# Turning normed rows, K and Q by VectorE blocks and SBUF transfers instead of TensorE

## The reference

```
# layers 0 and 1 (H = 16 and 8 heads), for each batch
xn = layernorm(x) * w + b
q, k, v = xn @ Wq + bq, xn @ Wk + bk, xn @ Wv + bv     # k masked by rows
q = softmax(q over a head's columns);  k = softmax(k over the 512 rows);  v = v * keep
attn = k^T v  per head;  y = q attn
x = x + silu(layernorm(y) * gain + shift) @ Wo + bo
# layer 2: softmax attention, 16 heads (not touched)
# layer 3: two norms and a modulation, then projections of the normed rows
#   (dlt, B, C, mx), then two state-space scans over 512 steps (not touched)
```

## Time and profile before

| | |
|---|---|
| median of three runs | 5686.29 us |
| the profiled execution | 5681.6 us |
| its span | 5679.5 us |
| TensorE, VectorE, ScalarE, GpSimd busy | 95%, 74%, 51%, 51% |
| layer 0, start of V of the first batch | 232.68 us |
| layer 1, start of V of the first batch | 840.14 us |
| front layer, first product | 2598.28 us |
| first product over the whole row with the scan | after 2915 us |

### The profile page before, as it was taken

How to read it: one execution, slowest core, us unless ns; L and a number is a source line. 1 busy time by engine, 2 the same in 40 slices (tenths; PEclk the granted TensorE clock), 3 DMA queues, 4 the chain that set the end, 5 groups by cost and what they waited for, 6 DMA issues and landing times. The chain is left out here.

```text
span 5679.5 us, 136465 instructions
## 1 busy us (share of the span) xinstructions
PE 5410.8 (95%) x58478; PEld 3262.1 (57%) x58478; DVE 4209.2 (74%) x5904; ACT 2919.1 (51%) x4944; POOL 2906.6 (51%) x956
## 2 busy tenths in 40 slices
PE   8999989998999999978989999999999999999998
PEld 3555545554455555544445566666666666666665
DVE  1456545554466666673349999999999999999996
ACT  0122212222455555551247776777777677677774
POOL 0000000000000000003449999999999999999997
PEclk9999999999999999998999999999999999999999
DMA  6200021001000000004431111112111121201211
GB/s 237 80 34 33 32 71 34 31 29 65 11 1 20 17 21 17 21 20 164 167 120 50 52 34 62 65 60 69 54 43 55 60 67 54 73 24 62 65 59 33
DMA packets 146330, 321.90 MB, mean 57 GB/s; under 512 B 27721, under 2 KB 28362, under 8 KB 135514
## 3 DMA queue, kind: packets, MB, share of 16 engines
q1 hardware_dynamic: 142866, 308.25, 16.1%
q10 hardware_dynamic: 2896, 5.34, 0.3%
HBM read 238.66 MB, written 74.89 MB: 55 GB/s over the span
## 5 line engine op out<-in xcount | busy, mean ns | idle before, releaser
L2070 POOL TENSOR_TENSOR sc_state<-sc_state,sc_c_rows 128x2048 f32<-128x2048 f32 x512 | 2330.2, 4564 | 122.8 <-DVE sc_state L2381 121.4
L2381 DVE TENSOR_TENSOR_SCAN sc_state<-sc_decay,wide 128x512 f32<-128x512 f32 x2048 | 2335.2, 1198 | 28.0 <-PE wide L2240 20.8
L2240 PEld LDWEIGHTS wide<-sc_diag,sc_du_t 64*64 64x64 f32 x32768 | 1048.0, 133 | 527.0 <-issue 344.0
L2240 PE MATMUL wide<-sc_diag,sc_du_t 64*64 64x128 f32 x32768 | 1218.9, 272 | 19.9 <-DVE sc_state L2381 19.7
L2256 PE MATMUL wide<-sc_state,half 64*64 64x512 f32 x8192 | 1199.5, 592 | 7.5 <-POOL sc_state L2070 7.0
L2174 ACT ACTIVATE sc_decay<-sc_delta,neg_a 128x512 f32<-128x512 f32 x1024 | 723.6, 719 | 448.7 <-DVE sc_state L2381 443.6
L2174 ACT ACTIVATE sc_decay<-sc_delta_x,neg_a 128x512 f32<-128x512 f32 x1024 | 710.1, 717 | 286.7 <-DVE sc_state L2381 282.5
L2256 PEld LDWEIGHTS wide<-sc_state,half 64*64 64x64 f32 x8192 | 405.8, 133 | 168.6 <-issue 127.5
L1491 DVE CUSTOM_DVE_ANT_0 l_prob<-wide,l_mask_add 128x512 f32<-128x512 f32 x512 | 339.6, 682 | 211.6 <-PE wide L1323 211.4
L1232 ACT ACTIVATE l_prob<-l_prob,l_s_max 128x512 f32<-128x512 f32 x512 | 366.0, 716 | 250.4 <-DVE l_s_max L1491 250.4
L2213 PE MATMUL wide<-set 128*128 128x512 f32 x1024 | 476.2, 608 | 0.0
(11 more groups left out here) (244 smaller groups left out, 6912.6 us busy)
## 6 DMA issues: line engine op xcount, KB each, us to landing
sc_c_rows<-c_d SPq DMA_DIRECT2D x64, 1024.0 KB, 4.8
set<-wz_tiles SPq DMA_DIRECT2D x128, 256.0 KB, 2.7
x<-ahead_out SPq DMA_DIRECT2D x24, 1024.0 KB, 4.8
ahead_x_wk<-x SPq DMA_DIRECT2D x16, 1024.0 KB, 5.7
sc_mx<-mx_d SPq DMA_DIRECT2D x64, 256.0 KB, 2.7
mx_d<-fr_mx SPq DMA_DIRECT2D x14, 1024.0 KB, 4.4
pro_wc<-in_wcT SPq DMA_DIRECT2D x4, 2048.0 KB, 19.2
xn_d<-fr_xn_t SPq DMA_DIRECT2D x8, 1024.0 KB, 4.2
```

Of the source, the lines that this page charges most:

```text
L2070: pool.tensor_tensor(state[quad % STATES][:, :, :], state[quad % STATES][:, :, :], c_rows[(r * 4 + q) % ROWS][:, :, :], ALU.mult).then_inc ...
L2240: last = pe.matmul(to[cols_to, k, :, :], du_t[slot % 2][rows, k, of * 64:(of + 1) * 64], diag[r % 2][rows, c, k, :, :], start=True, stop=True)
L2381: dve.tensor_tensor_scan(state[quad % STATES][:, step % 4, order], decay[step % DECAYS][:, order], pair[:, i, order], 0.0, ALU.mult, ALU.a ...
```

## The change

In layers 0 and 1, TK, TQ and T leave TensorE, except T of the very first batch. VectorE transposes the sixteen 32x32 blocks of each 128 columns in place of them (`turn_x`, `turn_k`, `turn_q`, four instructions of 128x512 each), and SyncE moves the blocks to their partitions by 16 SBUF to SBUF transfers of 64 KB (runs of 512 bytes) for each of the three (`move_x`, `move_k`, `move_q`). ScalarE's `next_norms` reads the moved rows from SBUF. The scaling of K by its sums is done in both layers and stands in `turn_k`, between K and Q on VectorE; `turn_q` stands between Q and O, `turn_x` after the norms. A goes to one bank and is masked by one instruction. The plan has 25 slots. Y reads every fourth column of `q_t`; the columns of Wk and bk are reordered on the host to suit. In the front layer the same is done to the normed rows of batches 1 to 7 (`move_blocks`, `scaled`, the latter after the silu of m = 5 of the batch before), and the additions to dlt, B and C (`drains`) come after the turning.

```diff
-        plan = [("V", 4, "dve"), ("TK", 4, "act"), ("TQ", 4, "act"), ("A", 4, "dve"), ("Y", 4, "dve"),
-                ("T", 4, "act"), ("K", 4, "dve"), ("TY", 4, "act"), ("Q", 4, "dve"), ("O", 4, "dve")]
+        plan = [("V", 4, "dve"), ("A", 1, "dve"), ("Y", 4, "dve"),
+                ("K", 4, "dve"), ("TY", 4, "act"), ("Q", 4, "dve"), ("O", 4, "dve")]
+        turn = (1, 2, 3, 0, 4) + (5, 6, 7, 0, 1, 2, 3, 4) * 2 + (5, 6, 7, 0)
...
+                def move_x(b):
+                    sp.wait_ge(x_turned, (b + 1) * TT)
+                    for i in range(4):
+                        for q in range(4):
+                            sp.dma_start(xn[q * 32:(q + 1) * 32, :, i * P:(i + 1) * P],
+                                         x_blocks[i * 32:(i + 1) * 32, q, :, :, :].rearrange("c k t r -> c k (t r)")
+                                         ).then_inc(x_moved, 16)
...  (move_k waits for k_turned and A of this batch, move_q for q_turned and Y of this batch)
                         load(b + 2, j)
+                        move_x(b)
+                        move_k(b)
+                        move_q(b)
                     sp.wait_ge(out_ready, (b + 1) * TT)
...
                 def next_norms(b):
+                    act.wait_ge(x_moved, (b + 1) * 256)
+                    act.wait_ge(psum_full, st.full(b, "V", TT - 1))
                     for k in range(DT):
-                        drain(b, "T", k, xn_t[:, k, :], ACT.Identity, scale=col(NW, k), bias=col(NB, k))
+                        act.activation(xn_t[:, k, :].rearrange("p (t i r) -> p t i r", t=TT, i=4),
+                                       xn[:, k, :].rearrange("p (i t r) -> p t i r", t=TT, i=4), ACT.Identity,
+                                       scale=col(NW, k), bias=col(NB, k)).then_inc(xn_t_ready, 1)
...  (TensorE)
-                        transposes(pe, b, "TK", k_t)
-                        transposes(pe, b, "TQ", q_tm)
                         pe.wait_ge(v_ready, (b + 1) * TT)
+                        pe.wait_ge(k_moved, (b + 1) * 256)
                         for g in range(DT):
...
-                                last_ins = pe.matmul(bank_of("A", g)[:, 0:P], lhs_t, rhs, start=(t == 0),
+                                last_ins = pe.matmul(bank_of("A", 0)[:, g * P:(g + 1) * P], lhs_t, rhs, start=(t == 0),
...
+                        pe.wait_ge(q_moved, (b + 1) * 256)
-                                                     q_t[:, g, t * P:(t + 1) * P], attn[:, g, :],
+                                                     q_t[:, g, t::TT], attn[:, g, :],
...  (VectorE)
+                def turn_x(b):
+                    for t in range(TT):
+                        dve.transpose(x_blocks[:, :, :, t, :].rearrange("p q k r -> p k q r"), xn[:, t, :]
+                                      ).then_inc(x_turned, 1)
+                def turn_k(b):
+                    dve.wait_ge(k_exp_ready, (b + 2) * DT)
+                    dve.reciprocal(k_sum[:, :], k_sum[:, :]).then_inc(rk_ready, 1)
+                    for k in range(DT):
+                        dve.tensor_scalar(k_t[:, k, :], k_t[:, k, :], k_sum[:, k:k + 1], None, ALU.mult)
+                    for k in range(DT):
+                        dve.transpose(k_blocks[:, :, :, :, k].rearrange("p q t r -> p t q r"), k_t[:, k, :])
...  (turn_q: dve.transpose(q_blocks[:, :, :, :, t] ..., q_tm[:, t, :]) after each exponential of Q)
+                        dve.tensor_tensor(attn[:, :, :], bank_of("A", 0)[:, :].rearrange("p (g n) -> p g n", g=DT),
+                                          block_mask[:, :].unsqueeze(1).broadcast_to([P, DT, P]), ALU.mult)
...
                     elif linear:
                         next_k(b)
+                        turn_k(b)
                         next_q(b)
+                        turn_q(b)
```

More of the change, by code:

```diff
@@ L424, in bank_of @@
         if linear:
-            return banks[(st.first[name] + k) % 8]
+            return banks[turn[st.first[name] + k]]
         return banks[(4 if name in ("V", "YT", "K", "Q") else 0) + k]
@@ L490, in attention_layer @@
         pt_full, pt_ready, pv_done, y_drained = sem("pt_full"), sem("pt_ready"), sem("pv_done"), sem("y_drained")
+        x_turned, x_moved, k_turned, k_moved = sem("x_turned"), sem("x_moved"), sem("k_turned"), sem("k_moved")
+        xn_t_ready, q_turned, q_moved = sem("xn_t_ready"), sem("q_turned"), sem("q_moved")
         def wait_bank(pe, b, name, k):
             if linear:
-                engine, count = st.before(b, name, k, 8)
-                pe.wait_ge(drained[engine], count)
+                at = st.first[name] + k
+                ring = next(r for r in range(1, st.n + 1) if turn[at - r] == turn[at])
+                engine, count = st.before(b, name, k, ring)
+                if not isinstance(count, int) or count > 0:
+                    pe.wait_ge(drained[engine], count)
             elif name in ("K", "TY", "Q", "O"):
@@ L782, in body @@
                 def body(b, pair, j, last):
[L783 to L788, removed]
+                    if not linear:
                         attention_act(act, b)
-                    if last:
-                        absent(st, act, drained["act"], "act", b, "T", 2)
-                    else:
+                    if not last:
                         next_norms(b)
@@ L958, in body @@
                     norms(b + 1, pair + j, 1 - j)
-                    if linear:
-                        dve.wait_ge(k_exp_ready, (b + 1) * DT)
-                        dve.reciprocal(k_sum[:, :], k_sum[:, :]).then_inc(rk_ready, 1)
-                        dve.wait_ge(rk_ready, b + 1)
-                        if layer == 0:
-                            for k in range(DT):
-                                dve.tensor_scalar(k_t[:, k, :], k_t[:, k, :], k_sum[:, k:k + 1], None, ALU.mult
-                                                  ).then_inc(k_norm_ready, 1)
+                    if not last:
+                        turn_x(b + 1)
                     for t in range(TT):
@@ L1029, in _ @@
                 dve.wait_ge(const_ready, 1)
+                turn_k(-1)
                 next_q(-1)
+                turn_q(-1)
                 absent(st, dve, drained["dve"], "dve", -1, "O", 1)
@@ L1631, in _, with move_blocks @@
                 load(1)
+                def move_blocks(b):
+                    sp.wait_ge(blocks_turned, b * TT)
+                    for i in range(4):
+                        for k4 in range(4):
+                            sp.dma_start(xn[b % 2][k4 * 32:(k4 + 1) * 32, :, i * P:(i + 1) * P],
+                                         turned[i * 32:(i + 1) * 32, k4, :, :, :].rearrange("c k t r -> c k (t r)")
+                                         ).then_inc(blocks_moved, 16)
                 for b in range(B):
@@ L1747, in _ @@
                             c_rows(b)
+                        if m == 5 and b + 1 < B:
+                            scaled(b + 1)
             @block.tensor
@@ L1865, in _ @@
                                           ALU.subtract, ALU.mult).then_inc(xn_ready, 1)
+                    if b >= 2:
+                        dve.wait_ge(blocks_moved, (b - 1) * 256)
+                    for t in range(TT):
+                        dve.wait_ge(xn_ready, b * TT + t + 1)
+                        dve.transpose(turned[:, :, :, t, :].rearrange("p j k r -> p k j r"), xn[j][:, t, :]
+                                      ).then_inc(blocks_turned, 1)
+                    drains(b - 1)
                 drains(B - 1)
@@ L2476, with by_fours @@
     s = lambda key: v["L3_cond_" + key]
+    def by_fours(layer, a):
+        return a if layer == 2 else a.reshape(a.shape[:-1] + (P, 4)).swapaxes(-1, -2).reshape(a.shape)
     def crossed(a):
```

156 lines of the change are left out of this document (107 added, 49 removed).

## The result

The changed kernel took 5729.64 us (median of four runs, 5728.98 to 5731.54), the kernel before beside it 5687.4 (5682.64 to 5688.97). The ratio is 1.0076, 95% interval 1.0059 to 1.0094. The forecast was 5608 with a range to 5672: the kernel is slower where faster was forecast. Its profiled execution has a span of 5727.9 us, 48.4 more than before.

What follows compares the result with a forecast made beforehand. TensorE was taken to set the period. Savings of 57.8 us in layers 0 and 1 and 20.1 in the front layer, together 77.9, off the median of 5686.3 gave 5608 us, with a range of 5588 to 5672.

Steps and rivals of the forecast that it cites:

- What bounds the kernel, and what goes: Steady batch: TensorE sets the period; 48 transposes and K's 1.64 us wait go, at its simplest 6.9 us per batch.
- Y at 3.68: On TensorE after A: Y starts 21.1 us after V's start and K could start 3.68 later, at 24.8.
- Rival B: Strided accesses: Y's weight loads at 192 ns make Y 6.1 us, strided transposes take 1.20; 5648 to 5669 us; chance 0.18.
- the store of the result, 1 us later than before, behind `move_q` ... cost zero: On SyncE's queue: GpSimd's `residual` still finds the store landed at 7.9; without that cover 1 us more in V's masking.
- A at 3.83: A on TensorE in a steady batch takes 3.83 us, from 16.3 to 20.1 after V's start.
- Transposes at 0.65: On VectorE: each 128x512 transpose takes 0.65 us, so `turn_x` ends 10.5 us after V's start; from above 1.20.
- Rival C: On VectorE: `turn_x` waits for GpSimd's `residual`, K starts at 27.7; 41 us in 14 batches, thus 5649; chance 0.08.
- The move of x in 9.1 us, ready at V + 22.7: SyncE's issues at 0.45 us, 2.3 to land, then ScalarE's scaling of 3.1; ready 2.1 us before K needs it.
- Rival D: Between `turn_x` and K on SyncE's queue: the move of x becomes the path; at 19.0 us, 40 slower, 5726; chance 0.10.
- First batches: First batch of layers 0 and 1: V ends at 22.0, K starts at 30.7; +0.4 and -1.8 us against before.
- Front layer: Layer ahead of the scan: 3.81 us less in each of six batches, batch 1 late by 2.8; gain 20.1 us.

Runs made afterwards that it cites:

- part (3): Theory that TensorE's wait in front of A lowers its clock and makes A long; tested by five spare matmuls behind V on the changed kernel: 5716.11 us.
- the fastest version: Changed kernel plus q's move on ScalarE's queue, q copied into token order, front-layer moves from batch 2, V's first tile masked early: 5606.35 us.

## Why the prediction was wrong

- *What bounds the kernel, and what goes*: right. TensorE set the period, the transposes and K's wait for ScalarE went, and nothing from K to the next V moved.
- *Y at 3.68*: the largest failure. The sum kept the duration of a load of neighbouring columns for one with a step of four. Rival B named it, but took the 192 ns of the earlier trace rows as the price at a step too; the load takes 329 ns, and Y 7.57 us where B had 6.1. That is 54 to 61 us. The sum had put the term at nothing; B had it, at 40, too small, and B's own time (5648 to 5669) would still have been faster than before.
- *"the store of the result, 1 us later than before, behind `move_q` ... cost zero"*: wrong. In this step the move was counted as one event; it is 16 issues of 0.65 us ahead of the store on one queue, so the store came 7 us later, at V + 8.5. By the prediction's own 0.45 per issue it would have been 7 us of queue. The chain store, `residual`, V's masking, A was known and written down, and the queue's length was not put into it. With the move of q on another queue, A came at V + 16.57 against the forecast 16.3. Worth 44 to 47 us, part (3) included.
- *A at 3.83*: held only where TensorE had not stood still for long. Before, TK and TQ filled the time between V and A, so the transposes did a second job: they kept the clock up (1.00 in the earlier trace rows). Taking work away from TensorE uncovered a wait, and the wait made the work behind it 1.4 to 2.9 us longer in 14 batches, 28 us in all. No rival had this.
- *Transposes at 0.65*: 0.62 for x, right. For K and Q 0.97 each in a row of four. In steady batches that is off the path: with Q's turning shortened the wait before A stayed at 2.67, and only in the first batches did it fall, from 8.8 and 9.0 to 7.5. Rival C (blocked by GpSimd): in the changed kernel `residual` came too late to stand beside `turn_x`; where it did stand there, with the move of q on ScalarE's queue, four transposes took 2.49 us. So C is out.
- *The move of x in 9.1 us, ready at V + 22.7*: too low. It took 13.0 from the end of `turn_x` (634.1) to ScalarE's start, as the loads stood ahead of it on the queue and each issue took 0.65 instead of 0.45; ready at V + 26.1. Rival D (slower through this move) did not decide anything in the changed kernel, since Y and A were late anyway. It does in the fastest version, at 1.2 us.
- *First batches*: A forecast at V + 22.2, measured at 22.9 in both layers. Right; with Y and A long, K came at V + 37.9 and 37.6.
- *Front layer*: the period right (3.91 less); batch 1 forecast 2.8 us late, 12 late in fact. VectorE's norms waited 10.1 us for GpSimd, which had `resid` ahead of them (3.0 before), and the move's issues took 10.3 us.

With the stride and the queue both mended 5632 remained, 24 above the forecast: the front layer is 8.5 of it, and in ten batches A still took 5.3 to 6.7 us, 20 us in all. The 5606 in the end is close to the forecast of 5608 by chance: that kernel has four edits that the prediction did not price (the queue, the copy, batch 1 of the front layer, V's first tile), and in it, too, A is long in four batches and K waits for the move. In short, the sum lacked two terms (the load's new duration, the lower clock behind a wait) and sized a third, the move's queue ahead of the store, as one event.

Open: why VectorE stood for 3.2 to 3.5 us in front of the mask in two batches of layer 0. Both begin an iteration of the loop over pairs of batches; the same batches of layer 1 show 0.63 us there, as does a batch of layer 0 in the kernel before. The trace names no cause, and no run was made for it.

## What to carry to other kernels

When work is taken off TensorE, ask what the work covered, and price the wait that it uncovers twice: once as a wait, and once as the matmuls behind it at the lower clock. When a transfer is cut into many, count its issues as a length of the queue, and walk everything behind them (here a store, a GpSimd addition, a VectorE masking) to the critical engine. An operand whose layout changes has a new duration: no row with the old layout is a price for it.

## What the runs showed of the hardware

- An fp32 weight load of 128 columns: 192 ns from neighbouring floats, 329 ns from every fourth one. A pair of load and 128-column matmul then goes at 0.237 us instead of 0.115, in the kernel with the transfers and in the one without, and also where the granted clock was 0.77.
- VectorE's 32x32 transposes of 128x512 fp32: 0.62 us each in a row of four into runs of 32 floats, 0.97 into a step of four floats. GpSimd's addition of 128x2048 beside the former did not hold them up (2.49 us for four).
- A transfer between partitions inside SBUF, 32 partitions with four runs of 512 bytes each: 0.65 us of issue on SyncE's queue, so 10.3 us for sixteen, and 10.4 to 13.1 us for sixteen on ScalarE's queue. They landed 2.0 us later for K and Q and 3.2 for x (medians, SyncE), 4.1 from ScalarE's queue.
- A burst of 32 matmuls of 128 columns (A, 3.83 us at full clock), in the 160 batches of the ten kernels that turn K and Q on VectorE: all 71 long ones (5.2 to 6.8 us) had a granted clock of 0.54 to 0.72, all 89 short ones (3.73 to 3.84) one of 1.00. The transfers don't tell them apart (a share of 0.15 to 0.89 beside long ones, 0 to 1.06 beside short ones). Every A behind a wait of 3.9 us or more was long, every one behind at most 2.25 short; of those behind 2.6 to 3.1 us, 17 were long and 17 short.
